# Row factors of the third graph layer computed on POOL as a power, with the engines' step order rewritten around it

## Chip, cores and metric

The kernel runs on one core of one Trainium2 chip. The metric is the device time of one execution in microseconds (us), lower is better. The engines are PE (matrix products and transposes), DVE (vector), ACT (activation functions), POOL (which here issues the indirect DMAs) and SP (which issues the direct DMAs).

## What is computed

Four graph layers follow one another on 50000 nodes of 128 features and 25000 edges, each followed by a residual sum and a normalisation over the features. The change touches the third layer (an attention layer whose own output is normalised once more before the residual):

```python
x_l = (x @ W_l + b_l).reshape(n, H, C)
x_r = (x @ W_r + b_r).reshape(n, H, C)
...
m = jax.nn.leaky_relu(x_j + x_r[tgt] + e_emb, NEG_SLOPE)
logits = jnp.einsum('ehc,hc->eh', m, att)
...
alpha = ex / (den[tgt] + 1e-16)
out = jax.ops.segment_sum(alpha[..., None] * x_j, tgt, num_segments=n)
...
out = jax.nn.gelu(out, approximate=False)
h = out + x
mu = jnp.mean(h, axis=-1, keepdims=True)
var = jnp.mean((h - mu) ** 2, axis=-1, keepdims=True)
return (h - mu) * jax.lax.rsqrt(var + LN_EPS) * ln_w + ln_b
```

## The kernel before

Every layer is a block of its own: the engines meet between layers. The third layer is `layer2`, and its tensors carry the prefix `g_` in the profile. Rows that belong to no layer of the change (`f_` is the last layer, `c_` the second) are not touched; the last layer, whose node pairs are loaded and scaled three steps ahead of its edges (`pairs_ahead = 3`), is the same text in both kernels.

`layer2` treats two kinds of rows. There are 49 node tiles of 1024 rows (two blocks of 512) and 49 edge tiles of 512 rows. Both are served by one loop over steps `c` from 0 to 63, written once for every engine, and each engine runs its instructions in exactly the order written; semaphores are the only other tie. In step `c` the node tile `g1 = c - 1` is activated by Gelu and centred, `g2 = c - 2` has its variance taken, and `g3 = c - 3` is scaled by its row factor, turned, given the affine weights and centred back. An edge tile is worked on twice: in step `c` its logits are computed as tile `c`, and eleven steps later (`lag = 11`) its softmax shares have come back from memory and it goes through the same Gelu, centre, scale, turn, affine chain as `e1 = c - 12` and `e3 = c - 14`. So there are three stretches: steps 0 to 10 with node tiles and edge logits only (here called the first stretch), steps 11 to 48 with everything (the joint stretch), and steps 49 to 63, the last of them (from 52) with edge tiles alone (the last stretch). Every seventh step has a part of the softmax in addition (`s1` and, one step later, `s2`).

The row factor is 1/sqrt(variance + eps). Per step ACT squares the centred rows (`sq1`, L1592), DVE adds the squares up (`var1`, `sums`, L1631), and ACT takes Ln and then Exp with scale -0.5 (`lnv1` L1608, `rstd1` L1613). Gelu and Ln/Exp are in different tables of ACT, so each step loads the Ln/Exp table (L1599) and, at the next Gelu, the Gelu table (L1558, in the last stretch L1563). ACT then multiplies the eight node row groups by their factors (`scale_block`, L1545) and DVE the edge block (`scaled`, L1627).

On PE a step is, in order: turn the node rows (L1405 into `psT`), the edge products (L1447, L1448), centre `gn` (L1410 into `psP`), centre `ge` (into `psU`), logits (L1471), turn the scaled nodes (L1405 `psT<-pre`), the second edge product (L1486), turn the scaled edges (L1405 into `psU` or `psZ`), centre the affine nodes (L1410 into `psP`), turn the next edge rows (L1405 `psT<-xd_xs`), centre the affine edges, node product (L1530). `turns` is one buffer of three blocks: `gn` and the affine node blocks use 0 and 1, `ge` and the affine edge block use 2.

POOL in `layer2` does nothing but issue eight indirect loads per step (L1332), `wait(pool, e_turned, now.n - 1)` ahead of them.

Of the kernel before, what the change touches and what calls it, by code (L numbers as in the profile page):

```python
# [1243 lines left out]
def layer2(nc, io, h):  # L1244
# [4 lines left out]
    with ExitStack() as ctx:  # L1249
# [25 lines left out]
        var1, lnv1, rstd1 = (sb(n, [P, 12]) for n in ("var1", "lnv1", "rstd1"))  # L1275
# [21 lines left out]
         ee_ready, pre1n_ready, pre1e_ready, sq1_ready, var1_ready, lnv1_ready, rstd1_ready, n1n_ready, n1e_ready, n1n_turned,  # L1297
# [6 lines left out]
             "pre1n_ready", "pre1e_ready", "sq1_ready", "var1_ready", "lnv1_ready", "rstd1_ready", "n1n_ready", "n1e_ready",  # L1304
# [9 lines left out]

        def edge_banks(c):
            return (psU[:, 0, :],) * 3 if c < STEPS else (psU[:, 0, :], psZ[:, 1, :], psZ[:, 0, :])
# [6 lines left out]
        def _(pool):  # L1323
            def step(t):
                now = t.tile(0)
                s = now.slot
                wait(pool, src_landed[s], 64 * now.half)
                wait(pool, dst_landed[s], 64 * now.half)
                wait(pool, e_turned, now.n - 1)
                for k, columns, landed in ((0, h.dst_row, dst_landed), (1, h.src_row, src_landed)):  # L1330
                    for j in range(4):
                        pool.indirect_dma_start(out=quarters(xd_xs[:, s, k, :])[j], out_offset=None, in_=table,  # L1332
                                                in_offset=edge_index(columns, now.n, j)).then_inc(landed[s], 16)

            run_steps(0, step)
# [66 lines left out]
        def _(pe):  # L1402
# [15 lines left out]

            def rows_of(dst, columns):
# [11 lines left out]
            for c in range(ends):  # L1431
                now, last = is_tile(c), is_tile(c - 1)
                g1, g3, e1, e3 = c - 1, c - 3, c - 1 - lag, c - 3 - lag
                sum_bank, turn_bank, out_bank = edge_banks(c)
# [15 lines left out]
                if is_tile(g1):  # L1450
# [3 lines left out]
                    ins.then_inc(en_ready, 1)  # L1454
                if is_tile(e1):
# [36 lines left out]
                if is_tile(e3):  # L1492
                    pe.wait_ge(n1e_ready, e3 + 1)
                    if c < STEPS:
                        pe.wait_ge(pre1e_ready, e1 + 1)
                    else:
                        pe.wait_ge(v_kept, STEPS)
                        wait(pe, affe_ready, e3)
                    turned_rows(turn_bank, pre1[:, g3 % 3, 2, :]).then_inc(n1e_turned, 1)
# [14 lines left out]
                if is_tile(e3):  # L1514
# [5 lines left out]
                    centred(out_bank, affT[:, 2, :]).then_inc(fe_ready, 1)  # L1520
# [14 lines left out]
        def _(act):  # L1535
# [15 lines left out]
            for c in range(ends):  # L1551
                now, last = is_tile(c), is_tile(c - 1)
                g1, g2, g3, e1, e2, e3 = c - 1, c - 2, c - 3, c - 1 - lag, c - 2 - lag, c - 3 - lag
                s1, (a, b) = run_at(c, runs + 1), blocks_of(g2)
# [5 lines left out]
                if is_tile(e1):  # L1560
                    act.wait_ge(agg_ready, e1 + 1)
                    wait(act, fe_ready, e1 - 2)
# [23 lines left out]
                if is_group(g2):  # L1586
                    if a == 0:
                        act.wait_ge(pre1n_ready, g2 + 1)
# [559 lines left out]
```

## Time and profile before

| | us |
|---|---|
| median of 3 runs | 3113.95 (3112.32 to 3114.8) |
| the profiled execution | 3120.47 |
| its span in the profile | 3118.6 |
| busy in it: PE, DVE, ACT, POOL | 2484.7, 2587.8, 2078.5, 1823.3 |

Busy is the time in which an engine worked on an instruction; the shares over the whole span average over four layers with different limits, so the prediction reads the stretches of `layer2` by themselves. In a timeline each row is an instruction or a run of equal ones: start, duration, engine, line, what it writes and reads, and in brackets how long the engine had been idle and what ended that.

### The profile page before, as it was taken

How to read it: one execution, taken by the hardware profiler on the slowest of the kernel's cores; microseconds unless marked ns; L12 is line 12 of the kernel's file. 1: busy time of each engine (PE TensorE's matmuls, PEld its weight loads, DVE VectorE, ACT ScalarE, POOL GpSimd, SP SyncE). 2: the span in 40 equal slices, each digit the busy share in tenths (PEclk: the TensorE clock that was granted, in tenths of full speed). 3: DMA queues.
4: the chain of work that ended last, by engine and by line, in shares of the span. 5: the costliest groups of instructions: out<-in, count | busy, mean ns of one | idle time of the engine just before them, and what ended most of it. 6: DMA issues, size and time to landing. Idle time of an engine off the chain costs nothing. (4 is left out here: it accounts for less than half of the span.)

```text
span 3118.6 us, 46608 instructions
## 1 busy us (share of the span) xinstructions
PE 2484.7 (80%) x14327; PEld 1752.4 (56%) x14327; DVE 2587.8 (83%) x3230; ACT 2078.5 (67%) x3724; POOL 1823.3 (58%) x1771
## 2 busy tenths in 40 slices
PE   7899999959999987888888589999999861435620
PEld 3466666637777765565666366777777651324420
DVE  6689999969999977999999557988999774999940
ACT  0167676736666656888888588999999863455520
POOL 4477777714434417777777365555555105777776
PEclk9999999979999998999999899999999955666765
DMA  7357676656777756777777447889988657995311
GB/s 211 117 168 225 219 223 220 221 166 203 218 219 219 218 168 203 236 233 230 231 232 231 126 139 186 214 201 234 225 219 203 179 147 230 296 283 165 95 53 39
DMA packets 495871, 611.80 MB, mean 196 GB/s; under 512 B 67257, under 2 KB 285827, under 8 KB 495500
## 3 DMA queue, kind: packets, MB, share of 16 engines
q1 hardware_dynamic: 433814, 495.64, 52.6%
q0 software_dynamic: 56480, 111.88, 13.8%
q8 instruction: 119, 1.95, 0.3%
q10 hardware_dynamic: 5334, 1.32, 0.2%
q14 instruction: 124, 1.02, 0.1%
HBM read 391.94 MB, written 220.55 MB: 196 GB/s over the span
## 5 line engine op out<-in xcount | busy, mean ns | idle before, releaser
L1332 POOL DMA_INDIRECT g_xd_xs<-table_x,dst_row x196 | 200.7, 1024 | 256.7 <-PE g_psT L1405 163.2
L781 POOL DMA_INDIRECT c_xs<-table_x,src_row x196 | 187.2, 955 | 261.0 <-PE c_psT L923 208.0
L1865 POOL DMA_INDIRECT f_rows<-table_x,src_row x196 | 191.3, 976 | 226.5 <-POOLq L1249 167.1
L771 POOL DMA_INDIRECT c_xs<-table_h,src_row x196 | 220.4, 1124 | 119.5 <-issue 78.8
L503 POOL DMA_INDIRECT xs<-in_x,src_i x196 | 227.1, 1159 | 86.2 <-issue 55.5
L488 POOL DMA_INDIRECT xd<-in_x,dst_i x196 | 216.5, 1105 | 95.0 <-issue 47.5
L1872 POOL DMA_INDIRECT out<-f_rows,end_i x196 | 196.5, 1003 | 66.5 <-issue 61.2
L1332 POOL DMA_INDIRECT g_xd_xs<-table_x,src_row x196 | 197.0, 1005 | 59.7 <-issue 59.7
L1916 PE MATMUL f_psT<-w_ident,f_rows 128*128 128x128 f32 x196 | 48.2, 391 | 219.8 <-DVE f_rows L2009 219.8
L771 POOL DMA_INDIRECT c_xd<-table_h,dst_row x196 | 185.0, 944 | 59.7 <-issue 59.7
L1410 PEld LDWEIGHTS g_psP<-w_center,g_turns 128*128 128x128 f32 x1568 | 186.0, 193 | 44.5 <-ACT g_turns L1558 27.6
L1410 PE MATMUL g_psP<-w_center,g_turns 128*128 128x128 f32 x1568 | 199.6, 281 | 6.1 <-ACT g_turns L1584 3.4
L1032 ACT ACTIVATE c_xo<-c_pre,c_rstd 128x128 f32<-128x128 f32 x588 | 182.0, 388 | 1.6
L1916 PEld LDWEIGHTS f_psT<-w_ident,f_rows 128*128 128x128 f32 x196 | 30.6, 194 | 232.2 <-DVE f_rows L2009 232.2
L1940 ACT ACTIVATE f_sqe<-f_rows 128x512 f32<-128x512 f32 x49 | 30.8, 630 | 159.6 <-DVE f_vare L1986 126.5
L953 PE MATMUL c_psV<-c_xsT,w_v 128*128 128x512 f32 x196 | 105.1, 618 | 35.6 <-DVE c_pv L1207 35.6
L1179 DVE TENSOR_TENSOR_SCAN c_m<-far,c_m,c_psA 128x512 f32<-128x512 bf16 x98 | 124.6, 1271 | 1.6 <-PE c_psA L958 1.6
L1410 PE MATMUL g_psU<-w_center,g_turns 128*128 128x128 f32 x672 | 100.9, 299 | 30.9 <-ACT g_turns L1563 30.9
L1213 DVE TENSOR_TENSOR_SCAN c_den<-c_c,c_den,c_p 128x512 f32<-128x512 f32 x96 | 122.2, 1273 | 0.0
L1219 DVE TENSOR_TENSOR_SCAN c_num<-c_c,c_num,c_pv 128x512 f32<-128x512 f32 x96 | 120.6, 1256 | 0.0
L1545 ACT ACTIVATE g_pre<-g_pre,g_rstd 128x128 f32<-128x128 f32 x392 | 119.3, 389 | 0.0
L1744 DVE TENSOR_TENSOR g_pre<-g_psP,g_xn 128x1024 f32<-128x1024 f32 x49 | 59.9, 1223 | 70.2 <-issue 39.0
(344 smaller groups left out, 8428.5 us busy)
## 6 DMA issues: line engine op xcount, KB each, us to landing
g_share<-shares SPq DMA_DIRECT2D x196, 192.0 KB
xn<-in_x SPq DMA_DIRECT2D x49, 512.0 KB
table_x<-xo SPq DMA_DIRECT2D x49, 512.0 KB
table_x1b<-xb SPq DMA_DIRECT2D x49, 512.0 KB, 4.9
c_xn<-table_x SPq DMA_DIRECT2D x49, 512.0 KB
table_h<-c_xo SPq DMA_DIRECT2D x49, 512.0 KB
c_xn<-table_h SPq DMA_DIRECT2D x49, 512.0 KB
c_x1r<-table_x1b SPq DMA_DIRECT2D x49, 512.0 KB
```

The costliest lines, as they stand in the source:

```text
L488: pool.indirect_dma_start(out=quarters(h.xd0[:, s, :])[j], out_offset=None, in_=io["x0"], in_offset=edge_index(h.dst_i, n, j)).then_inc(h. ...
L503: pool.indirect_dma_start(out=quarters(h.xs0[:, s, :])[j], out_offset=None, in_=io["x0"], in_offset=edge_index(h.src_i, n, j)).then_inc(h. ...
L771: pool.indirect_dma_start(out=quarters(rows[:, s, :])[j], out_offset=None, in_=table, in_offset=edge_index(columns, now.n, j)).then_inc(la ...
L781: pool.indirect_dma_start(out=quarters(xs[:, s, :])[j], out_offset=None, in_=table, in_offset=edge_index(h.src_row, now.n, j)).then_inc(sr ...
L1032: ins = nc.scalar.activation(quarters(xo[:, g.slot, j // 4, :])[j % 4], quarters(pre[:, g.slot, j // 4, :])[j % 4], ACT.Copy, scale=rstd[: ...
L1179: nc.vector.tensor_tensor_scan(m[:, s, 1:TILE + 1], h.far[:, here], psA[:, :], m[:, s, 0:1], ALU.add, ALU.max).then_inc(m_ready, 1)
L1213: nc.vector.tensor_tensor_scan(den[:, s, :], c[:, :], p[:, :], 0.0 if first else den[:, 1 - s, TILE - 1:TILE], ALU.mult, ALU.add).then_inc ...
L1219: nc.vector.tensor_tensor_scan(num[:, s, :], c[:, :], pv[:, :], 0.0 if first else num[:, 1 - s, TILE - 1:TILE], ALU.mult, ALU.add).then_in ...
L1332: pool.indirect_dma_start(out=quarters(xd_xs[:, s, k, :])[j], out_offset=None, in_=table, in_offset=edge_index(columns, now.n, j)).then_in ...
L1410: ins = nc.tensor.matmul(o, x, h.w["center"][:, :], start=True, stop=True)
L1865: pool.indirect_dma_start(out=quarters(rows[:, n, :])[j], out_offset=None, in_=table, in_offset=edge_index(h.src_row, n, j)).then_inc(src_ ...
L1872: pool.indirect_dma_start(out=io["out"], out_offset=edge_index(h.end_i, n, j), in_=quarters(rows[:, n, :])[j], in_offset=None, bounds_chec ...
```

## The change

The row factors of `layer2` are computed on POOL: `mean = var / 128 + eps`, then `mean` to the power -0.5 against a tile filled with -0.5. ACT's Ln and Exp of each step go, and with them the table loads, except around the softmax's Exp every seventh step. The square is taken one step earlier on ACT (tile `g1` at the end of its step instead of `g2`), the sums on DVE come before the first node sum instead of after the last, ACT scales the nodes first in its step, and in the steps that have edges alone PE turns the scaled edges ahead of the centring of `ge`, while the affine edge block goes to block 0 of `turns`. POOL issues the loads of tile `n` and then the factors of group `n - 4`, and its first loads now wait for `att_ready`.

```diff
         @block.gpsimd
         def _(pool):
-            def step(t):
-                now = t.tile(0)
-                s = now.slot
-                wait(pool, src_landed[s], 64 * now.half)
-                wait(pool, dst_landed[s], 64 * now.half)
-                wait(pool, e_turned, now.n - 1)
+            def gather(n):
...
+                wait(pool, e_turned, n - 1)
...
-            run_steps(0, step)
+            def factors(g, a, b):
+                pool.wait_ge(var1_ready, g + 1)
+                wait(pool, rstd1_ready, g)
+                nc.gpsimd.tensor_scalar(mean1[:, 4 * a:4 * b], var1[:, 4 * a:4 * b], 1.0 / P, EPS, ALU.mult,
+                                        ALU.add).then_inc(mean1_ready, 1)
+                pool.wait_ge(mean1_ready, g + 1)
+                wait(pool, n1n_ready, min(g, STEPS))
+                wait(pool, n1e_ready, g - lag)
+                nc.gpsimd.tensor_tensor(rstd1[:, 4 * a:4 * b], mean1[:, 4 * a:4 * b], minus_half[:, 4 * a:4 * b],
+                                        ALU.pow).then_inc(rstd1_ready, 1)
+
+            pool.wait_ge(att_ready, 1)
+            for n in range(STEPS + lag + 4):
+                if is_tile(n):
+                    gather(n)
+                if is_group(n - 4):
+                    factors(n - 4, *blocks_of(n - 4))
...
+                if is_tile(e3) and c >= first_alone:
+                    turn_sums(c)
                 if is_tile(e1):
                     pe.wait_ge(ge_ready, e1 + 1)
...
-                    centred(out_bank, affT[:, 2, :]).then_inc(fe_ready, 1)
+                    centred(out_bank, affT[:, affine_block(c), :]).then_inc(fe_ready, 1)
...
+                if is_tile(g3):
+                    act.wait_ge(rstd1_ready, g3 + 1)
+                    scale_block(g3, 0)
+                    scale_block(g3, 1).then_inc(n1n_ready, 1)
                 if is_tile(g1):
                     act.wait_ge(y_ready, g1 + 1)
...
-                    wait(act, fe_ready, e1 - 2)
+                    wait(act, fe_ready, min(e1 - 2, first_alone - 3 - lag))
+                    wait(act, ee_ready, e1)
                     nc.scalar.activation(ge[:, :], agg[:, e1 % 2, :], ACT.Gelu, bias=h.col("g_bias")).then_inc(ge_ready, 1)
-                if is_tile(g3):
-                    act.wait_ge(rstd1_ready, g3 + 1)
-                    scale_block(g3, 0)
-                    scale_block(g3, 1).then_inc(n1n_ready, 1)
...
-                if is_group(g1) and is_group(g2):
-                    nc.scalar.preload_act_table_set(LN_EXP)
+                if is_group(g1):
...
+                    nc.scalar.activation(sq1[:, a:b, :], pre1[:, g1 % 3, a:b, :], ACT.Square).then_inc(sq1_ready, 1)
                 if s1 is not None:
                     act.wait_ge(args_ready, s1 + 1)
+                    nc.scalar.preload_act_table_set(LN_EXP)
                     nc.scalar.activation(expo[:, :, :], expo[:, :, :], ACT.Exp).then_inc(exps_ready, 1)
...
-                    nc.scalar.activation(lnv1[:, 4 * a:4 * b], var1[:, 4 * a:4 * b], ACT.Ln, bias=h.eps[:, :],
-                                         scale=1.0 / P).then_inc(lnv1_ready, 1)
...
-                    nc.scalar.activation(rstd1[:, 4 * a:4 * b], lnv1[:, 4 * a:4 * b], ACT.Exp,
-                                         scale=-0.5).then_inc(rstd1_ready, 1)
...
+            nc.vector.memset(minus_half[:, :], -0.5)
...
+                if is_group(g2):
+                    dve.wait_ge(sq1_ready, g2 + 1)
+                    wait(dve, mean1_ready, g2)
+                    sums(var1[:, 4 * a:4 * b], sq1[:, a:b, :], var1_ready)
                 if is_tile(g1):
                     wait(dve, n1n_turned, g1 - 2)
...
-                if is_group(g2):
-                    dve.wait_ge(sq1_ready, g2 + 1)
-                    wait(dve, lnv1_ready, g2)
-                    sums(var1[:, 4 * a:4 * b], sq1[:, a:b, :], var1_ready)
```

`first_alone` is 52, and `affine_block(c)` is 2 before that step and 0 from it on.

ACT in one joint step without a softmax part, before, from the copy of the edge rows on:

```order
L1541 ACTIVATE g_edgeT<-g_psT 128x1024
L1608 ACTIVATE g_lnv<-g_var,eps 128x12
L1613 ACTIVATE g_rstd<-g_lnv 128x12
L1558 ACT_TABLE_LOAD
L1558 ACTIVATE g_turns<-g_psP,bl_out 128x1024
L1563 ACTIVATE g_turns<-g_agg,cols 128x512
L1545 ACTIVATE g_pre<-g_pre,g_rstd 128x128 x8
L1571 ACTIVATE g_nodeT<-g_psT 128x1024
L1575 ACTIVATE g_values<-g_psZ,cols 128x1024
L1580 ACTIVATE g_alike<-g_psA 128x256
L1584 ACTIVATE g_turns<-g_psT,cols 128x1024
L1592 ACTIVATE g_sq<-g_pre 128x1536
```

The same of the changed kernel, with its own line numbers:

```order
L1567 ACTIVATE g_edgeT<-g_psT 128x1024
L1571 ACTIVATE g_pre<-g_pre,g_rstd 128x128 x8
L1588 ACTIVATE g_turns<-g_psP,bl_out 128x1024
L1594 ACTIVATE g_turns<-g_agg,cols 128x512
L1598 ACTIVATE g_nodeT<-g_psT 128x1024
L1602 ACTIVATE g_values<-g_psZ,cols 128x1024
L1607 ACTIVATE g_alike<-g_psA 128x256
L1611 ACTIVATE g_turns<-g_psT,cols 128x1024
L1620 ACTIVATE g_turns<-g_psU,cols 128x512
L1628 ACTIVATE g_sq<-g_pre 128x1536
```

Ln, Exp and the load are gone between the edge copy and the Gelu, and the scaling of the nodes stands ahead of the Gelu.

DVE in a joint step, before, from the last sum of one step (L1807) on; L1744 is the first node sum and L1787 the second:

```order
L1807 TENSOR_TENSOR g_pre<-g_psU,g_x2e 128x512
L1730 TENSOR_TENSOR g_values<-g_values,g_share 128x1024
L1627 TENSOR_TENSOR g_pre<-g_pre,g_rstd 128x512
L1739 TENSOR_TENSOR g_values<-g_values 128x512
L1744 TENSOR_TENSOR g_pre<-g_psP,g_xn 128x1024
...
L1787 TENSOR_TENSOR g_pre<-g_psP,g_xn 128x1024
L1631 TENSOR_REDUCE g_var<-g_sq 128x12
L1796 SCALAR_TENSOR_TENSOR g_zsl<-g_low 128x512
```

The same place in the changed kernel (L1769 and L1812 are the two node sums):

```order
L1828 TENSOR_TENSOR g_pre<-g_psU,g_x2e 128x512
L1647 TENSOR_TENSOR g_pre<-g_pre,g_rstd 128x512
L1754 TENSOR_TENSOR g_values<-g_values,g_share 128x1024
L1760 TENSOR_TENSOR g_values<-g_values 128x512
L1651 TENSOR_REDUCE g_var<-g_sq 128x12
L1769 TENSOR_TENSOR g_pre<-g_psP,g_xn 128x1024
...
L1812 TENSOR_TENSOR g_pre<-g_psP,g_xn 128x1024
L1817 SCALAR_TENSOR_TENSOR g_zsl<-g_low 128x512
```

The sum of squares has moved from behind the second node sum to ahead of the first.

PE in steps that have edge tiles alone, two steps before:

```order
L1410 MATMUL g_psU<-w_center,g_turns 128x128 x4
L1405 MATMUL g_psZ<-w_ident,g_pre 128x128 x4
L1410 MATMUL g_psZ<-w_center,g_turns 128x128 x4
L1410 MATMUL g_psU<-w_center,g_turns 128x128 x4
L1405 MATMUL g_psZ<-w_ident,g_pre 128x128 x4
L1410 MATMUL g_psZ<-w_center,g_turns 128x128 x4
```

and in the changed kernel:

```order
L1425 MATMUL g_psZ<-w_ident,g_pre 128x128 x4
L1430 MATMUL g_psU<-w_center,g_turns 128x128 x4
L1430 MATMUL g_psZ<-w_center,g_turns 128x128 x4
L1425 MATMUL g_psZ<-w_ident,g_pre 128x128 x4
L1430 MATMUL g_psU<-w_center,g_turns 128x128 x4
L1430 MATMUL g_psZ<-w_center,g_turns 128x128 x4
```

The turn of the scaled edges now stands ahead of the centring of `ge`.

## Rows read from the trace of the kernel before

**Rows 1.** Windows: the three stretches; busy us (instructions) per engine, granted clock, DMA.

```profile
1780.00:1910.00 130.00, 116.13 (x714) 78.85 (x713) 73.10 (x104) 109.38 (x170) 85.68 (x89) 1.00 0.47 140
1937.00:2451.00 514.00, 499.67 (x3333) 369.10 (x3332) 459.53 (x619) 475.83 (x741) 277.77 (x270) 1.00 0.88 218
2470.00:2595.00 125.00, 75.51 (x347) 63.47 (x346) 76.88 (x112) 72.06 (x108) 0.00 (x0) 0.60 0.50 129
```

**Rows 2.** Groups of instructions, 1775 to 2595 us: busy, mean ns, idle before.

```profile
L1599 ACT ACT_TABLE_LOAD x59 | 75.7, 1283 | 1.1
L1558 ACT ACT_TABLE_LOAD x48 | 61.6, 1283 | 1.0
...
L1608 ACT ACTIVATE g_lnv<-g_var,eps 128x12 f32<-128x12 f32 (+2 forms) x60 | 18.1, 302 | 46.9 <-DVE g_var L1631 46.8
```

**Rows 3.** Timeline of one joint step: start, us, engine, line.

```profile
2223.95 2.05 PE L1410 MATMUL g_psP<-w_center,g_turns 128*128 128x128 f32 x16
...
2226.11 1.22 DVE L1787 TENSOR_TENSOR g_pre<-g_psP,g_xn 128x1024 f32<-128x1024 f32 x1 [1.00 <-PE g_psP L1410]
...
2227.25 1.74 DVE L1631 TENSOR_REDUCE g_var<-g_sq 128x12 f32<-128x1536 f32 x1
...
2229.59 1.28 ACT L1558 ACT_TABLE_LOAD   x1
...
2230.89 1.11 ACT L1558 ACTIVATE g_turns<-g_psP,bl_out 128x1024 f32<-128x1024 f32 x1
...
2235.95 1.06 PE L1405 MATMUL g_psT<-w_ident,g_pre 128*128 128x128 f32 x8 [0.39 <-issue]
...
2237.06 1.20 ACT L1584 ACTIVATE g_turns<-g_psT,cols 128x1024 f32<-128x1024 f32 x1
...
2238.31 2.05 PE L1410 MATMUL g_psP<-w_center,g_turns 128*128 128x128 f32 x16
```

**Rows 4.** Timeline of ACT: the Gelu of steps 11, 12 and 49.

```profile
1910.11 1.11 ACT L1558 ACTIVATE g_turns<-g_psP,bl_out 128x1024 f32<-128x1024 f32 x1
...
1923.32 1.12 ACT L1558 ACTIVATE g_turns<-g_psP,bl_out 128x1024 f32<-128x1024 f32 x1
...
2464.59 1.11 ACT L1558 ACTIVATE g_turns<-g_psP,bl_out 128x1024 f32<-128x1024 f32 x1
```

**Rows 5.** Timeline: POOL's loads of one joint step, and DVE beside them.

```profile
2183.65 0.94 POOL L1332 DMA_INDIRECT g_xd_xs<-table_x,dst_row  x1 [5.11 <-PE g_psT L1405]
...
2186.91 1.22 DVE L1730 TENSOR_TENSOR g_values<-g_values,g_share 128x1024 f32<-128x1024 f32 x1
...
2187.51 1.43 POOL L1332 DMA_INDIRECT g_xd_xs<-table_x,dst_row  x1 [0.30 <-issue]
...
2193.00 1.17 POOL L1332 DMA_INDIRECT g_xd_xs<-table_x,src_row  x1 [0.30 <-issue]
```

**Rows 6.** Timeline of the last stretch: one step, and sums L1807 of steps 51 and 60.

```profile
2508.66 0.68 DVE L1807 TENSOR_TENSOR g_pre<-g_psZ,g_x2e 128x512 f32<-128x512 f32 x1
...
2555.54 1.28 ACT L1563 ACT_TABLE_LOAD   x1 [0.36 <-PE g_psZ L1410]
...
2557.61 2.08 PE L1410 MATMUL g_psU<-w_center,g_turns 128*128 128x128 f32 x8 [2.15 <-ACT g_turns L1563]
...
2560.58 0.78 ACT L1596 ACTIVATE g_turns<-g_psZ,cols 128x512 f32<-128x512 f32 x1 [2.50 <-PE g_psZ L1405]
...
2563.57 1.28 ACT L1563 ACT_TABLE_LOAD   x1 [0.36 <-PE g_psZ L1410]
...
2579.65 0.69 DVE L1807 TENSOR_TENSOR g_pre<-g_psZ,g_x2e 128x512 f32<-128x512 f32 x1 [2.53 <-PE g_psZ L1410]
```

**Rows 7.** Timeline: the start of the layer, and POOL's operation of before.

```profile
0.94 0.34 POOL L425 IOTA i_rev_row<- 98x256 int32 x1
...
1756.83 0.94 POOL L1332 DMA_INDIRECT g_xd_xs<-table_x,dst_row  x1 [42.24 <-POOLq L789]
...
1757.91 0.17 DVE L1708 COPY g_att_a<-att_m 128x4 f32<-128x4 f32 x1
```

More of the change, by code:

```diff
@@ L1274, in layer2 @@
         gn, ge, affT = turns[:, 0:2, :], turns[:, 2, :], turns
-        var1, lnv1, rstd1 = (sb(n, [P, 12]) for n in ("var1", "lnv1", "rstd1"))
+        var1, mean1, rstd1, minus_half = (sb(n, [P, 12]) for n in ("var1", "mean1", "rstd1", "minus_half"))
         far, reach = sb("far", [P, runs, chunk], BF16), sb("reach", [P, runs, chunk])
@@ L1313, in is_group, with affine_block @@
             return 0 <= g < STEPS + lag
+        first_alone = STEPS + 3
+        def affine_block(c):
+            return 2 if c < first_alone else 0
         def edge_banks(c):
@@ L1323, in _ @@
         def _(pool):
-            def step(t):
-                now = t.tile(0)
-                s = now.slot
-                wait(pool, src_landed[s], 64 * now.half)
-                wait(pool, dst_landed[s], 64 * now.half)
-                wait(pool, e_turned, now.n - 1)
+            def gather(n):
+                s = n % 2
+                wait(pool, src_landed[s], 64 * (n // 2))
+                wait(pool, dst_landed[s], 64 * (n // 2))
+                wait(pool, e_turned, n - 1)
                 for k, columns, landed in ((0, h.dst_row, dst_landed), (1, h.src_row, src_landed)):
@@ L1417, in turn_edges, with turn_sums @@
                 turned_rows(psT[:, 1, :], xd_xs[:, n % 2, 1, :]).then_inc(e_turned, 1)
+            def turn_sums(c):
+                e1, g3, e3 = c - 1 - lag, c - 3, c - 3 - lag
+                pe.wait_ge(n1e_ready, e3 + 1)
+                if c < STEPS:
+                    pe.wait_ge(pre1e_ready, e1 + 1)
+                else:
+                    pe.wait_ge(v_kept, STEPS)
+                    wait(pe, affe_ready, e3)
+                turned_rows(edge_banks(c)[1], pre1[:, g3 % 3, 2, :]).then_inc(n1e_turned, 1)
             def rows_of(dst, columns):
@@ L1491, in _ @@
                     rows_of(psA[:, 0, :], [c_here[:, chunk - 1:chunk], d_here[:, chunk - 1:chunk]]).then_inc(d_rows, 1)
[L1492 to L1499, printed above, removed]
+                if is_tile(e3) and c < first_alone:
+                    turn_sums(c)
                 if s1 is not None:
@@ L1726, in _ @@
                     running_maximum(s1)
+                if is_tile(e3):
+                    dve.wait_ge(rstd1_ready, g3 + 1)
+                    scaled(pre1[:, g3 % 3, 2:3, :], pre1[:, g3 % 3, 2:3, :], rstd1[:, 8:12], 1, n1e_ready)
                 if is_tile(e0):
@@ L1730, in _ @@
                     nc.vector.tensor_tensor(v, v, share[:, e0 % 2, 1:3, :], ALU.mult).then_inc(weighed, 1)
-                if is_tile(e3):
-                    dve.wait_ge(rstd1_ready, g3 + 1)
-                    scaled(pre1[:, g3 % 3, 2:3, :], pre1[:, g3 % 3, 2:3, :], rstd1[:, 8:12], 1, n1e_ready)
                 if s2 is not None:
```

38 lines of the change are left out of this document (17 added, 21 removed).

## The prediction

> **What bounds the kernel now.** I read the windows of the third layer first, because the change lies wholly inside it, then the groups of instructions for what each edit removes, then the timeline of one step per stretch, to find the loop of waits that sets the step. [rows 1] are the three stretches. In the joint stretch PE is busy 499.7 of 514 us (97%), ACT 93%, DVE 89%, POOL 54%: three engines are nearly full, so taking time from one of them is worth only the distance to the next. In the first stretch PE has 89%, ACT 84%, DVE 56%. In the last, no engine has over 62%, and the granted clock is 0.60, that is mostly the lower level of 1.2 GHz: this stretch is a chain of waits, and PE's products in it cost twice.
>
> The steps come from [rows 4]: 13.21 us in the first stretch (step 11 to 12), and (2464.59 - 1923.32) / 37 = 14.63 us in the joint one. [rows 3] show what sets it. From the start of the second node centring (PE, 2223.95) it goes to the second node sum on DVE (2226.11), to the sum of squares (2227.25, 1.74 us), to Ln and Exp on ACT, to the table load (2229.59, 1.28 us), to the Gelu (2230.89), through ACT's scaling and copies to the affine activation (2237.06), and to the same PE instruction (2238.31): 14.36 us, closed without a gap worth naming. ACT's mean wait for the sum of squares is 46.9 / 60 = 0.78 us a step [rows 2]. So in the joint stretch the loop is PE, DVE, ACT in turn, with PE just under it.
>
> **What the change does, part by part.**
>
> Ln, Exp and the loads. 59 + 48 loads of 1.283 us and 11 more at the edge Gelu [rows 2, 6] become one pair per softmax run, 14 in all with the first Gelu counted; with Ln at 0.30 and Exp at about two thirds of that, ACT loses some 3.1 us a step and its wait of 0.78. In the joint stretch ACT falls from 13.5 to about 10.6 us a step, so it no longer bounds. The loop above is cut in two places: the sum of squares is no longer between the node sum and the next Gelu, and the factor gets a step of slack on POOL.
>
> What takes over in the joint stretch. PE is next. As the windows count it, it is busy 0.972 x 14.63 = 14.2 us a step [rows 1, 4], which leaves 0.4 us at most. That busy time has slack in it that the profile hides, since ends are modelled: the turn of the scaled nodes waited at 2235.95 for ACT's node copy (0.39 us idle [rows 3]), and ACT gets there about two us earlier in the new order, because the scaling no longer sits behind a load. Below is 13.2 us, DVE's 0.89 x 14.63 = 13.1 and a little for its semaphores; above is 14.36, no gain. I take 13.95 for a step without a softmax part, 0.4 less. Three of seven steps carry or feel the softmax parts, which are chains on DVE, and I give them 0.25. (4 x 0.4 + 3 x 0.25) / 7 = 0.34 us, times 37 steps: -13 us.
>
> POOL's two operations. No row shows a tensor operation of POOL with inputs. From below: its iota took 0.34 us [rows 7], twice that is 0.7. From above: an indirect DMA takes it up to 1.43 us when something holds it up, [rows 5], twice that and two waits of 0.3 are 3.5 us. 128 x 12 elements are a small load and nearer to the iota; I take F = 1.6 us for both with their waits. In the joint stretch POOL issues its loads in 10.5 us (2183.65 to 2194.17) and had then waited 5.11 us for PE [rows 5], so 1.6 lies in that idle time. What waits for the factor is ACT's scaling, first in its next step, and behind it everything on ACT; the sums are ready long before the loads are all issued, so the factor is there 10.5 + 1.6 = 12.1 us after the loads began and about two us before ACT wants it.
>
> First stretch. Its step could fall to PE's 0.89 x 13.21 = 11.8 us [rows 1, 4]. But POOL needs 10.5 + 0.3 + 1.6 = 12.4 us there, as the factors stand in the same queue, somewhat less where loads aren't stretched. I take 12.3, a gain of 0.9 over nine steps: -8 us.
>
> Last stretch. Step 51 to 60 are nine steps in 2579.65 - 2508.66 = 71.0 us, 7.9 each. [rows 6] show one: load 1.28, Gelu, PE 2.08, turn, ACT 0.78, PE 2.08, load again, 8.03 in all. The ring closes because Gelu and affine edges share a block of `turns`; the change gives them two, turns first, and loads nothing. What stays is edge scaling on DVE (0.68 by the same shape as L1807), turn 0.9 (2559.69 to 2560.58), two PE groups of 2.08 behind each other, and the last sum 0.69: 6.4 us. That is 1.5 x 9 = -13.5. At the higher clock PE's two groups would halve and DVE's own work would bound the step near 5.5; at no gain it stays 7.9. In steps 49 to 51, from 2464.59 [rows 4] to 2508.66 [rows 6], 44.1 us, the path loses a load (1.28), Ln and Exp (0.5) and the sum of squares (1.74): 3.5 each, -10.5. Together -24.
>
> The costs. The first loads wait for `att_ready`: the copy that gives it ends at 1758.08, the loads began at 1756.83 [rows 7], and PE's first turn waits for them: +1.3 us, with nothing to hide it. The extra memset of DVE is under 0.1. One more configuration instruction of POOL stands ahead of its first factor; POOL's start in this layer, which has one too, was 0.6 us behind the others, and it falls into idle time.
>
> Sum: -13 - 8 - 24 + 1.3 = -44 us. The profiled execution was 3120.5 (span 3118.6), 6.5 above the median of the runs, so it goes to about 3076, and the median from 3114 to **3070**.
>
> **A rule that speaks against it.** The long load of 1.43 us in [rows 5] against 0.94 for its neighbours lies beside L1730, a DVE product of two operands in SBUF: so POOL and DVE disturb one another here already. The Trainium skill, "SBUF — State Buffer", section "Who interferes with whom", says that a DVE instruction with two SBUF inputs and a GpSimd instruction that reads SBUF exclude each other for a whole instruction. The new POOL operations read SBUF, the loads' descriptors mostly write. By that rule either side can be held: this is the second rival.
>
> **Rivals.**
> 1. POOL's power is dear, and the kernel gets slower. The place is POOL's queue: a step can't be shorter than 10.8 + F. Speaking for it: a power isn't a simple operation, and no row prices it. Against: only 12 elements per partition. With F = 5.3 (two operations, each 1.43 and held by a DVE product of 1.22 us [rows 5]) the step is 16.1 in both stretches: (16.1 - 14.6) x 37 + (16.1 - 13.2) x 9 = +81; in the last stretch, where 3.3 us lie between sum and scaling, its nine steps gain nothing and -8 remains. +74: 3188. It decides from F = 4 on: 9 x 1.6 + 37 x 0.15 + 1 - 18 is about +3.
> 2. POOL and DVE exclude each other. F stays small, but each joint step loses about 1 us of DVE, which has 1.5 us to spare and has it at other places. Then the joint stretch gains nothing or loses 0.7 x 37 = 26, and the rest gives its 31: 3083 to 3109, a case that can end within what counts as no change.
> 3. PE alone bounds the joint stretch, as its busy share says: 14.2 us is all it gives, with nothing in softmax steps, 0.1 x 37 = 4. Then -35: 3079, nearly the forecast.
> 4. More than forecast: DVE's 13.3 us becomes the joint step and the last stretch keeps the higher clock: -37 - 33 - 12 = -80: 3034.
>
> **How the numbers follow.** Forecast with rival 3: 0.72; rival 4 or near it 0.09; rival 2 0.09, a third of it within 0.2%; rival 1 0.10, nearly all slower. 0.2% is 6 us, about what a measurement of this kernel can tell from no change. Faster 0.86, same 0.04, slower 0.10. The range 3038 to 3106 leaves out rival 1 and the tips of 2 and 4.
>
> **What would show it.** ACT loads of the layer fall from 118 to 15 or less. POOL shows two short operations per step with a sum under 2 us, and its queue doesn't end the wait of ACT's scaling. The joint step is near 14.3 us on average and PE stays at 0.97 busy or more; the first stretch near 12.3 with POOL nearly without idle time; the last near 6.4 a step. I am wrong if POOL's operations take over 3.5 us, if DVE's products beside them lengthen, or if PE's groups in the joint stretch turn out to have more hidden waiting than 0.4 us a step.

## The result, and the profile after

The changed kernel takes 3101.67 us (median of 5 runs, 3096.52 to 3104.76) beside 3113.95 for the kernel before on the same chip: ratio 0.995, 95% interval 0.9939 to 0.9961. Measured again on another chip it took 3095.95 beside 3113.71: 0.9941, interval 0.9928 to 0.9955. So it is 12 to 18 us faster where 44 were forecast.

The third layer, from its first table load to that of the layer behind it, took 838.9 us in the profile of before and 816.1 after. By parts, marked by the starts of the node Gelu (n-th tile) and of the last edge node sum, in us:

| part of the layer | before | forecast | after | both again |
|---|---|---|---|---|
| start to Gelu 1 | 25.51 | +1.3 | 27.95 (+2.4) | 25.67, 27.87 |
| Gelu 1 to 3 | 21.42 | with the next | 29.52 (+8.1) | 21.46, 30.05 |
| Gelu 3 to 12 | 120.20 | -8 | 119.34 (-0.9) | 120.22, 119.24 |
| Gelu 12 to 49 (37 joint steps) | 541.27 | -13 | 534.65 (-6.6) | 541.26, 534.43 |
| Gelu 49 to the last edge sum | 126.09 | -24 | 100.23 (-25.9) | 123.82, 101.09 |

The rest of the layer is 4.43 us in both. The windows of [rows 1] after the change, at the same times and with the same columns:

```profile
1780.00:1910.00 130.00, 109.44 (x650) 73.42 (x649) 67.65 (x98) 81.31 (x131) 97.59 (x99) 0.95 0.40 123
1937.00:2451.00 514.00, 497.59 (x3364) 370.94 (x3362) 461.21 (x622) 391.28 (x613) 406.27 (x351) 1.00 0.91 220
2470.00:2595.00 125.00, 63.75 (x371) 57.09 (x370) 87.53 (x121) 47.90 (x70) 32.80 (x42) 0.74 0.66 175
```

ACT's busy time in the joint stretch fell from 93% to 76%, POOL's rose from 54% to 79%, and PE stayed at 97%, but less was won than ACT gave up. The groups of instructions in the layer, ACT's table loads against [rows 2] and POOL's new operations:

```profile
L1588 ACT ACT_TABLE_LOAD x7 | 9.0, 1283 | 0.1
L1631 ACT ACT_TABLE_LOAD x7 | 9.0, 1283 | 13.3 <-DVE g_expo L1687 13.3
...
L1347 POOL TENSOR_TENSOR g_rstd<-g_mean,g_minus_half 128x12 f32<-128x12 f32 x38 | 91.1, 2396 | 3.2
L1347 POOL TENSOR_TENSOR g_rstd<-g_mean,g_minus_half 128x8 f32<-128x8 f32 x11 | 18.3, 1667 | 0.9
L1342 POOL TENSOR_SCALAR g_mean<-g_var 128x12 f32<-128x12 f32 x38 | 11.1, 293 | 38.7 <-DVE g_var L1651 37.7
L1347 POOL TENSOR_TENSOR g_rstd<-g_mean,g_minus_half 128x4 f32<-128x4 f32 x11 | 11.1, 1007 | 0.9
```

The loads are gone as forecast (16 left). But the seven that remain before the softmax's Exp have 13.3 us of waiting for DVE ahead of them, and the power takes 2.40 us for 12 columns: F is 2.40 + 0.29 and gaps, 3.0 us, against 1.6 forecast.

The first loss is at the third Gelu, 20.34 us behind the second where it had been 11.22. ACT, and the end of POOL's queue before it (start, duration, ..., idle time and what ended it):

```profile
1804.40 1.02 ACT L1567 ACTIVATE g_edgeT<-g_psT 128x1024 f32<-128x1024 f32 x1 [1.59 <-PE g_psT L1425]
1814.10 2.44 ACT L1571 ACTIVATE g_pre<-g_pre,g_rstd 128x128 f32<-128x128 f32 x8 [8.68 <-POOL g_rstd L1347]
1816.45 1.09 ACT L1588 ACTIVATE g_turns<-g_psP,bl_out 128x1024 f32<-128x1024 f32 x1
```
```profile
1803.49 0.94 POOL L1336 DMA_INDIRECT g_xd_xs<-table_x,dst_row  x1 [0.30 <-issue]
...
1811.01 0.95 POOL L1336 DMA_INDIRECT g_xd_xs<-table_x,src_row  x1 [0.30 <-issue]
1812.08 0.22 POOL L1342 TENSOR_SCALAR g_mean<-g_var 128x8 f32<-128x8 f32 x1
1812.39 1.68 POOL L1347 TENSOR_TENSOR g_rstd<-g_mean,g_minus_half 128x8 f32<-128x8 f32 x1
```

On DVE the sums of the first tile had been ready since 1796.23:

```profile
1795.02 1.21 DVE L1651 TENSOR_REDUCE g_var<-g_sq 128x8 f32<-128x1024 f32 x1
```

POOL comes to them 15.9 us later, behind the loads of the fifth tile, and ACT, which scales first in its step, holds everything back until then.

The second loss is in each softmax step of the joint stretch, 17.3 to 17.8 us long where it had been 15.63. A softmax step on ACT in the kernel before, with the load done by the time DVE's exponents came:

```profile
2180.89 1.28 ACT L1599 ACT_TABLE_LOAD   x1
2182.43 0.48 ACT L1602 ACTIVATE g_expo<-g_expo 128x336 f32<-128x336 f32 x1 [0.26 <-DVE g_expo L1667]
```

and one after:

```profile
2190.05 1.47 ACT L1628 ACTIVATE g_sq<-g_pre 128x1536 f32<-128x1536 f32 x1
2192.96 1.28 ACT L1631 ACT_TABLE_LOAD   x1 [1.44 <-DVE g_expo L1687]
2194.26 0.48 ACT L1632 ACTIVATE g_expo<-g_expo 128x336 f32<-128x336 f32 x1
...
2195.55 2.44 ACT L1571 ACTIVATE g_pre<-g_pre,g_rstd 128x128 f32<-128x128 f32 x8
2198.00 1.28 ACT L1588 ACT_TABLE_LOAD   x1
2199.30 1.11 ACT L1588 ACTIVATE g_turns<-g_psP,bl_out 128x1024 f32<-128x1024 f32 x1
```
```profile
2200.47 1.72 PE L1430 MATMUL g_psP<-w_center,g_turns 128*128 128x128 f32 x13 [1.70 <-ACT g_turns L1588]
```

ACT waits 1.44 us for DVE's exponents with the old table in, and loads only then. Behind that stand the scaling (2.44), the second load and the Gelu, and PE waits 1.70 us for the Gelu. The 37 joint steps hold five softmax steps. These five and the five that follow them took 153.0 us before and 156.5 after, so they lost 3.4 us; the other 27 steps, called ordinary here, went from 388.3 to 378.2 and won 10.1.

The ordinary steps could have won more. The factor, which was to be ready two us before ACT wants it, is ready just as ACT takes it: in 20 of the 37 joint steps ACT's scaling starts less than 0.1 us behind the power, and nine times from 1940 to 2400 ACT had waited for it, 7.4 us in all. One of these nine, with POOL's power ahead of it, and the row of the waits (us in total, times, longest):

```profile
2074.43 2.29 POOL L1347 TENSOR_TENSOR g_rstd<-g_mean,g_minus_half 128x12 f32<-128x12 f32 x1
2076.76 2.45 ACT L1571 ACTIVATE g_pre<-g_pre,g_rstd 128x128 f32<-128x128 f32 x8 [0.78 <-POOL g_rstd L1347]
```
```profile
ACT g_pre L1571 <- POOL g_rstd L1347: 7.4, 9, 1.3
```

### The profile page after: what moved, and what is told of

Its sections match the earlier page's. It is cut to its first block and busy times, and to the rows that moved or that the text cites. A ratio compares the mean times of both kernels' runs of the same rounds, so it can differ in the third digit from the quotient of the medians.

```text
span 3099.9 us, 46510 instructions
## 1 busy us (share of the span) xinstructions
PE 2460.4 (79%) x14327; PEld 1739.5 (56%) x14327; DVE 2586.2 (83%) x3231; ACT 1926.8 (62%) x3501; POOL 1987.3 (64%) x1891
## 5 line engine op out<-in xcount | busy, mean ns | idle before, releaser
L1336 POOL DMA_INDIRECT g_xd_xs<-table_x,dst_row x196 | 226.4, 1155 | 122.6 <-issue 57.7
L1571 ACT ACTIVATE g_pre<-g_pre,g_rstd 128x128 f32<-128x128 f32 x392 | 119.6, 389 | 16.4 <-POOL g_rstd L1347 16.1
L1347 POOL TENSOR_TENSOR g_rstd<-g_mean,g_minus_half 128x12 f32<-128x12 f32 (+2 forms) x60 | 120.5, 2008 | 5.0
L1769 DVE TENSOR_TENSOR g_pre<-g_psP,g_xn 128x1024 f32<-128x1024 f32 x49 | 59.8, 1221 | 69.3 <-issue 52.7
```

## The experiments

The ratios are to the kernel before on the same chip; times of parts come from each run's own trace.

**1. The table load ahead of the wait.**

```diff
-                    act.wait_ge(args_ready, s1 + 1)
                     nc.scalar.preload_act_table_set(LN_EXP)
+                    act.wait_ge(args_ready, s1 + 1)
```

> The changed kernel with one line moved: in each of the seven softmax steps ACT loads the Ln/Exp table before it waits for DVE's arguments instead of after. Theory A (the loads of the softmax steps stand on the path: such steps took 17.3 to 17.8 us in the joint stretch against 15.6 before the change, and ACT stood idle 1.44 us for DVE before the load at 2192.96): each of the seven steps loses up to 1.28 us, the kernel 6 to 9 us, to about 3094, and the row of the load no longer has idle time for DVE ahead of it. Rival B (POOL's queue sets these steps too, so ACT's time is free): within 2 us of the changed kernel.

3091.57 us, ratio 0.9921 (0.9904 to 0.9937). The same step on ACT:

```profile
2184.74 1.47 ACT L1628 ACTIVATE g_sq<-g_pre 128x1536 f32<-128x1536 f32 x1
2186.23 1.28 ACT L1630 ACT_TABLE_LOAD   x1
2187.56 0.48 ACT L1632 ACTIVATE g_expo<-g_expo 128x336 f32<-128x336 f32 x1
```

The softmax steps fall to 16.1 to 16.6 us, the one in the first stretch from 16.02 to 14.74, the joint stretch to 529.58. Wait and load now run side by side: the idle time of 1.44 us is gone. Theory A holds. In the joint stretch the softmax steps and their followers win 7.0 us, 1.4 per softmax step, and the ordinary steps give 1.9 of it back, with ACT waiting for POOL's factor ten times, 9.3 us.

**2. The first two factors ahead of the loads of tiles 4 and 5.**

```diff
             for n in range(STEPS + lag + 4):
+                if n in (4, 5):
+                    factors(n - 4, *blocks_of(n - 4))
                 if is_tile(n):
                     gather(n)
-                if is_group(n - 4):
+                if is_group(n - 4) and n not in (4, 5):
```

> The changed kernel, but POOL computes the factors of groups 0 and 1 before the loads of tiles 4 and 5 instead of after them. Theory C (the first factors queue behind five tiles of loads: ACT stood idle 8.68 us for them, and step 2 to 3 took 20.3 us against 11.2 before): ACT's wait falls under 1 us, and the kernel loses 7 to 9 us, to about 3093. Rival D (POOL is behind from the start and the time lost there only moves: the loads of tiles 4 and 5 come late instead, since POOL issues one tile in 10 us and has to wait for the sums): 0 to 3 us gained.

3100.59 us, 0.9951 (0.9934 to 0.9967). The stall isn't gone; it stands two steps later. POOL's operations without its loads:

```profile
1799.52 0.74 POOL L1342 TENSOR_SCALAR g_mean<-g_var 128x8 f32<-128x8 f32 x1
1800.34 1.68 POOL L1347 TENSOR_TENSOR g_rstd<-g_mean,g_minus_half 128x8 f32<-128x8 f32 x1
1812.67 0.22 POOL L1342 TENSOR_SCALAR g_mean<-g_var 128x8 f32<-128x8 f32 x1
1812.98 1.68 POOL L1347 TENSOR_TENSOR g_rstd<-g_mean,g_minus_half 128x8 f32<-128x8 f32 x1
1835.85 0.20 POOL L1342 TENSOR_SCALAR g_mean<-g_var 128x8 f32<-128x8 f32 x1
```

The third factor comes 23 us after the second, since two tiles' loads now stand between them, and ACT waits 8.4 us for it. Gelu 1 to 12 takes 148.7 us (148.9 in the changed kernel, 141.6 before). So it isn't a matter of the first factors: with loads ahead of factors in POOL's queue, the layer pays once for a factor that comes a tile's loads late, wherever the order begins. Rival D was right.

**3 and 4. The power's price: a product in its place, and the power twice.** The third run multiplies where the power should be, so its row factors aren't those of the reference; the fourth computes one more power into a spare tile that nobody reads.

```diff
-                                        ALU.pow).then_inc(rstd1_ready, 1)
+                                        ALU.mult).then_inc(rstd1_ready, 1)
```

> The changed kernel with the power replaced by a product, so the row factors are wrong and the output with them; instructions, waits and order are the same. It prices the power (2.4 us for 12 columns, 1.67 for 8, 1.01 for 4). Theory E (POOL's queue bounds first and joint stretch: eight loads 10.8 us and 3.0 us for the factors): a product takes about 0.3 us, a step of POOL falls by 2.1 us, and the joint step falls from 14.45 to PE's 13.6 to 14.0 on average, the first stretch from 12.72 to 11.8 to 12.2 a step, together -20 to -35 us, to 3065 to 3082. Rival F (PE alone bounds the joint stretch, POOL has room): -5 to -12, from the first stretch and the first factors alone.

```diff
+                nc.gpsimd.tensor_tensor(spare[:, 4 * a:4 * b], mean1[:, 4 * a:4 * b], minus_half[:, 4 * a:4 * b], ALU.pow)
                 nc.gpsimd.tensor_tensor(rstd1[:, 4 * a:4 * b], mean1[:, 4 * a:4 * b], minus_half[:, 4 * a:4 * b],
```

> The changed kernel with a second power of the same size into a spare tile ahead of the real one; the output is unchanged. Theory E (POOL bounds): the 37 joint steps grow by nearly the whole 2.4 us, the first stretch by 1.7 a step, together +90 to +110 us, to about 3200, and POOL waits for PE nowhere. Rival F (POOL has slack): the slack is used up first, +30 to +60.

With the product: 3092.51 us, 0.9932 (0.9914 to 0.9949). Its price, by groups:

```profile
L1347 POOL TENSOR_TENSOR g_rstd<-g_mean,g_minus_half 128x12 f32<-128x12 f32 x38 | 11.8, 311 | 3.2
```

2.1 us less a step gives only 534.65 - 530.93 = 3.7 us over 37 joint steps: the ordinary ones win 5.3, those with and after a softmax part lose 1.6. ACT waits for POOL's factor nowhere in the joint stretch and mostly takes it some 2 us after it is ready, and most ordinary steps come to 13.70 us, with PE counted busy throughout. The steps without softmax in the first stretch stay at 12.7, and the third Gelu is still late (18.84 us). Rival F is about right: PE's own 13.70 lies just under what POOL allowed, so the power itself took little. With two powers: 3172.23 us, 1.0181 (1.0164 to 1.0198), joint stretch 598.56. One step of POOL in it:

```profile
2084.51 1.59 POOL L1336 DMA_INDIRECT g_xd_xs<-table_x,dst_row  x1 [0.18 <-issue]
...
2096.29 0.22 POOL L1342 TENSOR_SCALAR g_mean<-g_var 128x12 f32<-128x12 f32 x1
2096.59 2.30 POOL L1345 TENSOR_TENSOR g_spare<-g_mean,g_minus_half 128x12 f32<-128x12 f32 x1
2098.88 2.32 POOL L1348 TENSOR_TENSOR g_rstd<-g_mean,g_minus_half 128x12 f32<-128x12 f32 x1
2101.38 1.49 POOL L1336 DMA_INDIRECT g_xd_xs<-table_x,dst_row  x1 [0.18 <-POOL g_rstd L1348]
```

Here POOL has no idle time beyond the 0.2 to 0.3 us between its instructions; 12 us of loads and 5 of factors make most ordinary steps 15.8 to 16.9 us. The second power costs 63.9 / 37 = 1.7 us a step of its 2.3, and in the ordinary steps alone 2.2, nearly all of it: in the changed kernel POOL had next to no room in them, and PE's 13.70 was just beneath. Theory E is right on what sets these steps; its +90 to +110 us was too high, the layer grew by 75.

**5. The last stretch's order undone.**

```diff
-        first_alone = STEPS + 3
+        first_alone = 2 * STEPS
...
-                            act.wait_ge(ee_ready, e1 + 1)
+                            act.wait_ge(ee_ready, min(e1 + 1, STEPS))
```

> Two parts of the change for the last stretch are undone: the turn of the edge sums stands again behind the other turns, and the affine edges keep one block. The loads and the sum of squares stay gone. The last stretch took 126.1 us before and 100.2 in the changed kernel. Theory G (the -26 us come mostly from the loads, Ln, Exp and the sum of squares that left the path): it stays within 5 us of 100, the kernel near 3105. Rival H (the ring through the shared block, one load in each step of 8.03 us, has to be cut as well): a step is 8.03 - 1.28 = 6.75 against the 5.6 measured, so +12 us over eleven steps, the kernel near 3114, as slow as the one before.

3105.22 us, 0.9965 (0.9951 to 0.9979). The stretch takes 108.25 us, 8.0 more than in the changed kernel, between G's 5 and H's 12. Seven of its steps are 6.73 to 6.75, H's number. PE and ACT in one, then in the changed kernel:

```profile
2532.55 0.78 ACT L1620 ACTIVATE g_turns<-g_psZ,cols 128x512 f32<-128x512 f32 x1 [3.03 <-PE g_psZ L1425]
...
2533.38 2.08 PE L1430 MATMUL g_psZ<-w_center,g_turns 128*128 128x128 f32 x8 [0.87 <-ACT g_turns L1620]
...
2536.35 2.05 PE L1430 MATMUL g_psU<-w_center,g_turns 128*128 128x128 f32 x8 [0.90 <-ACT g_turns L1594]
```
```profile
2535.12 1.06 PE L1430 MATMUL g_psU<-w_center,g_turns 128*128 128x128 f32 x8
2535.32 0.78 ACT L1620 ACTIVATE g_turns<-g_psZ,cols 128x512 f32<-128x512 f32 x1 [1.18 <-PE g_psZ L1425]
...
2536.15 1.05 PE L1430 MATMUL g_psZ<-w_center,g_turns 128*128 128x128 f32 x7
```

In the old order each centring waits 0.9 us for ACT and lasts 2.05 to 2.08; in the new one, PE goes from one to the next, and part of them last 1.05. The granted clock from 2475 to 2575 is 0.61 there and 0.77 in the changed kernel. So of the 25.9 us, 18 come from the loads, Ln, Exp and the square, and 8 from the order. The 8 are rather 4 to 8: from the sum of step 51 to the last one it took 62.6 us in the changed kernel, 62.9 to 66.4 in the other kernels with the new order and 63.6 in the second profile of the changed one, against 70.4 here.

**6. The attention wait behind the first loads.**

```diff
-            pool.wait_ge(att_ready, 1)
             for n in range(STEPS + lag + 4):
+                if n == 4:
+                    pool.wait_ge(att_ready, 1)
```

> POOL's wait for the attention copy stands ahead of its first factors and not ahead of its first loads. The time from the layer's start to its first Gelu was 25.5 us before and 27.95 in the changed kernel. Theory I (the wait ahead of the loads costs all of that): -2.4 us, the first Gelu 25.5 us after the start. Rival J (the first Gelu waits for other parts of the layer's start too): under 1 us. The total can hardly show it; the time to the first Gelu does.

Start to first Gelu 26.59 us, 1.36 less and still 1.1 more than before: between I and J. The wait costs what the prediction gave it (1.3); what makes the other 1.1 stays open. The whole (3096.07 us, 0.9938, 0.9918 to 0.9957) can't show it.

**7. Gelu ahead of the scaling, on top of run 1.**

```diff
-                if is_tile(g3):
-                    act.wait_ge(rstd1_ready, g3 + 1)
-                    scale_block(g3, 0)
-                    scale_block(g3, 1).then_inc(n1n_ready, 1)
...
+                if is_tile(g3):
+                    act.wait_ge(rstd1_ready, g3 + 1)
+                    scale_block(g3, 0)
+                    scale_block(g3, 1).then_inc(n1n_ready, 1)
```

> On top of the load ahead of the wait (3091.6 us): ACT computes the node and edge Gelu first and scales the older tile's nodes behind it, as the kernel before did. Theory K (PE's centring waits for the Gelu 23 times, 21.8 us in 450, and the scaling of 1.2 to 2.4 us stands ahead of it): the Gelu comes earlier by the scaling, the joint stretch loses up to 20 us, the kernel goes to 3075 to 3085. Rival L (the step hangs on the scaling, through the turn and the affine copies to PE, which in the first stretch waits 1.26 us a step for them): the first stretch goes from 12.7 to near 13.2 a step, and the joint one gains nothing or loses up to 0.5 a step: 3095 to 3112.

3084.24 us, 0.9897 (0.9878 to 0.9916); the joint stretch takes 522.63 us, 7.0 less than in run 1, the layer 803.1 (810.5 in run 1). Most steps without a softmax part are 13.69 to 13.70, and the softmax steps 15.5:

```profile
2176.17 1.28 ACT L1630 ACT_TABLE_LOAD   x1
2177.59 0.48 ACT L1632 ACTIVATE g_expo<-g_expo 128x336 f32<-128x336 f32 x1
...
2179.00 1.28 ACT L1584 ACT_TABLE_LOAD   x1
2180.82 1.11 ACT L1584 ACTIVATE g_turns<-g_psP,bl_out 128x1024 f32<-128x1024 f32 x1 [0.54 <-PE g_psP L1556]
```

Now the Gelu waits for PE's product, not PE for the Gelu. Theory K's number comes, and L's loss in the first stretch doesn't (12.7 a step as before). But K's reason isn't where the gain lies. The 21.8 us that it starts from belong to PE's weight loads; PE itself waited 7.8 us for the Gelu. And by kinds of steps, in us (the second profiles gave 153.0 and 388.2 for the kernel before, 155.8 and 378.6 for the changed one):

| joint stretch | softmax steps and the steps after them (10) | ordinary (27) |
|---|---|---|
| before | 153.0 | 388.3 |
| changed | 156.5 | 378.2 |
| load ahead of the wait (run 1) | 149.5 | 380.1 |
| product (run 3) | 158.0 | 372.9 |
| two powers (run 4) | 162.1 | 436.4 |
| Gelu ahead of the scaling (run 7) | 150.6 | 372.0 |

Against run 1 the softmax steps win nothing (the step falls to 15.5, the one after it grows from 13.6 to 14.6); all of the gain, 8.1 us, is in the ordinary steps. There ACT had waited 9.3 us for POOL's factor in run 1; now the scaling comes later in ACT's step, finds the factor about 2 us old or older, and never waits. The product, with the old order on ACT, reaches the same 13.70 a step. So a factor that comes earlier and a scaling that comes later give the same, and what the ordinary steps had lost was the wait for the factor.

**8. Factors ahead of the loads in every step** (on the changed kernel alone).

```diff
             for n in range(STEPS + lag + 4):
-                if is_tile(n):
-                    gather(n)
                 if is_group(n - 4):
                     factors(n - 4, *blocks_of(n - 4))
+                if is_tile(n):
+                    gather(n)
```

> In every step POOL computes the factors ahead of that step's loads, and not only at the start. Theory M (the 9.1 us that the third Gelu waits come from one tile's loads of some 9 to 10 us that stand between sum and factor, once, and with the order turned they never do): -9 us, 3093, the wait doesn't come back later, since the next loads are always behind a factor that is ready. Rival N (POOL then waits for each sum with its loads unissued, and the tiles arrive later): steps of the first stretch grow from 12.7 towards 14 and the joint ones by what POOL waits: 3100 to 3130.

3098.21 us, 0.9943 (0.9924 to 0.9962). Both are right, each in its stretch: Gelu 1 to 12 falls from 148.9 to 142.1 us, and the joint stretch grows from 534.7 to 540.5. The last stretch varies besides, and the layer takes 818.5 us, 2.4 more than in the changed kernel.

**9 and 10. All four edits together; and with factors ahead only for tiles up to 15.** Runs 1, 6, 7 and 8 in one kernel, and the same with this loop:

```diff
+                if is_tile(n) and n > 15:
+                    gather(n)
                 if is_group(n - 4):
                     factors(n - 4, *blocks_of(n - 4))
-                if is_tile(n):
+                if is_tile(n) and n <= 15:
                     gather(n)
```

> Four edits together: load ahead of the wait, Gelu ahead of the scaling, the attention wait behind the first loads, and factors ahead of loads in every step. The first three alone should give 3084.2 - 1.4 = 3082.8. The fourth gave -6.8 us between Gelu 1 and 12 and +5.8 in the joint stretch. Theory O (the +5.8 is POOL's own and stays): 3082, joint stretch 528. Rival P (the +5.8 came from ACT's order, scaling ahead of the Gelu, and is gone with it): 3076, joint stretch 523.

> As the run of four edits, but factors stand ahead of loads only up to the sixteenth tile, and behind them from there. Under theory O this keeps the -6.8 and pays no 5.8, but once a stall where the order turns over, since two tiles' loads then stand ahead of one factor: up to 5 us. That gives 3076 to 3081, and it beats the run of four edits by 1 to 6 us. Under rival P it is behind that run by the stall, 0 to 5 us.

All four: 3088.49 us, 0.9918 (0.9906 to 0.993), joint stretch 534.80, 12.2 more than in run 7, so worse than O, and P falls. Two rows of its waits from 1940 to 2400 (us in total, times, longest):

```profile
POOL g_mean L1342 <- DVE g_var L1652: 28.0, 20, 2.8
...
PE g_psT L1426 <- DMA g_xd_xs<-table_x,src_row: 10.2, 9, 1.9
```

The changed kernel has neither row in that stretch: here POOL waits for sums with its loads unissued, and PE then waits for the loads. The tenth: 3079.98 us, 0.9884 (0.9869 to 0.9899), the lowest of all. Gelu 1 to 12 is 3.7 us shorter than in run 7 and the joint stretch 4.4 longer, with one step of 20.0 us where the order turns over. Run 7 has 12.75 us from the tenth Gelu to the eleventh, this run 18.64, in which PE waits 4.06 us for a tile's loads to land; the ninth, in the same order up to there, had 13.43, so why isn't shown. In time it can't be told from run 7 (layer 801.3 against 803.1).

**11 and 12. Both kernels again, for second profiles.**

> The kernel before itself, for a second profile of it. The third layer, from its first table load to that of the layer behind it, took 838.9 us in the first profile and 816.1 in that of the changed kernel, -22.8, while the medians are only 12.3 us apart. In the eight profiles of other versions the median minus the layer's time lies between 2278.7 and 2281.6 (2285.5 for the changed one), and for the kernel before it is 2275.0. Theory Q (the first profile of before caught a layer some 6 us slower than usual): 833 us now. Rival R (the layer takes 839 always and another part of the kernel is what differs between profile and median): 838 to 840, and the rest of the span 5 us shorter than the 2279.7 of the first profile.

> The changed kernel itself, for a second profile and a measurement beside the kernel before on one chip. Theory Q: the layer takes 816 us again, within 1.5, and the ratio is 0.995, within 0.0015. Rival S (its layer varies from execution to execution as well): 819 us or more.

The kernel before: layer 836.9 us, its parts in the table above, ratio to itself 1.0006 (0.9997 to 1.0015). Q falls, the layer wasn't slow by chance; R holds for the layer, but the rest of the span was 2283.1, not 5 us shorter. The changed kernel: 817.1. Gelu 1 to 49 repeats within 0.4 us in both; what varies is the last stretch (2.3 us in the kernel before) and the other layers. The profiled execution of before was each time some 6 us above its median (3120.5, 3121.8), that of the changed kernel at its median; why, stays open. In the second measurement layer and whole agree: 3115.98 and 3095.95 us are 20.0 apart, the layers 19.7. In the first they don't, 12.3 against 22.8. So the layer's gain is 20 to 23 us, and how much of it arrives in the whole is known only as 12 to 20.

## Why the prediction failed, step by step

**The first stretch: -8 forecast, +7.2 measured (Gelu 1 to 12).** The step that failed is "POOL needs 10.5 + 0.3 + 1.6 = 12.4 us there": a rate was worked out and no start. The sentence that "the factor is there 10.5 + 1.6 = 12.1 us after the loads began and about two us before ACT wants it" takes for granted that the sums are ready long before the loads are all issued and POOL is abreast; at the layer's beginning POOL's queue is a tile's loads behind the sum. That cost 8.1 us, and runs 2 and 8 show that the order in POOL's queue is the cause. From Gelu 3 to 12 only 0.9 us were won of the 8: the step after the stall was 1.4 longer than before, the softmax step 1.6 (run 1 takes 1.3 of that back), and the other seven won 3.9, about 0.5 each where 0.9 was forecast. Their steady length came to 12.7, not 12.3, with F = 2.3 for 8 columns, and POOL doesn't set it: with the product, and with ACT's order turned (run 7), it is 12.75 as well. In all three PE is busy 11.7 us of it, waits 0.43 for the affine activation (L1611) and 0.60 for the second node sum (L1812), and each of these two had itself just waited for PE. So it is PE with two short round trips, 11.7 + 1.03; no run took them out.

**The joint stretch: -13 forecast, -6.6 measured.** With the two orders on ACT turned back it gives 541.27 - 522.63 = 18.6 us (run 7), at a steady 13.70 against 13.95 forecast, so the 97% of PE did hide more waiting than the 0.4 us that I gave it (rival 3, PE's floor at 14.2, is refuted). Two steps failed. The first is "three of seven steps carry or feel the softmax parts, ... and I give them 0.25": the softmax step got 1.7 to 2.2 us longer, and with the step after it the five lost 3.4 us in place of a gain of 2.5. The diff showed why and I gave it no price: the preload moved from ahead of the wait to behind it, 1.4 us a softmax step, 7.0 in the stretch by run 1, which is more than the whole loss. The second is the sentence on the factor, "about two us before ACT wants it": loads and factors took POOL 13.1 to 14.6 us in nearly every joint step and not 12.1 (F was 1.4 more, and eight loads took up to 11.8 where one step's 10.5 had been read), ACT's scaling stood first in a shorter step, and the two us were gone; of the signs that I had named, POOL's queue did end waits of ACT's scaling. That cost the ordinary steps 5 to 6 us (runs 3 and 7). Their 10.1 us still met the forecast for them (about 10), and that is luck: the floor of PE was lower than I said by about as much as the wait for the factor took.

**F: 1.6 forecast, 3.0 measured.** A mis-sized term. A power costs much more than a product (2.40 against 0.31 us), which the iota couldn't show. It stayed under the point of 4 us from which rival 1 decides, and was worth 3.7 us. Rival 1's formula was right for the joint stretch: with two powers F is about 5.3, and its step of 16.1 was met by 16.2 on average. Its 3188 against 3172 is less exact: the first stretch, with 8 columns, had steps of 13.6 to 14.0, and the last one won 22 us where rival 1 left 8.

**The last stretch: -24 forecast, -25.9 and -22.7 measured.** The total is right and its mechanism too (run 5: without the new order steps are 6.75, and the loads, Ln, Exp and the square are worth 18), but the two terms in it were each off: -10.5 forecast and -6.5 measured up to the sum of step 51, -13.5 forecast and -19.4 measured behind it, where I left out the last two steps and where eleven steps of 4.1 to 6.75 came in place of 6.4. The shortest have products of 1.05 us, the length at the higher clock, which was rival 4's part. That the two errors cancel is luck.

**The layer's start: +1.3 forecast, +2.4 measured.** The term that I priced is right (1.36 by run 6); another 1.1 us isn't explained.

Together: +1.1 for the start, +15.2 for the first stretch, +6.4 for the joint, -1.9 for the last make 20.8 us of the 21 between -44 and the layer's -22.8. The rest to the medians lies outside the layer and stays open: I took the 6.5 us by which the profiled execution stood over the median to be in both kernels, and it was not.

**Rival 2, POOL and DVE holding each other.** DVE's sums and products keep their times beside a power; the power doesn't. Two of them in the changed kernel, the first with the DVE product of two SBUF tensors (`g_ew`, `g_values`) that runs as it starts:

```profile
2017.10 0.72 DVE L1788 SCALAR_TENSOR_TENSOR g_zw<-g_ew,cols,g_values 128x512 f32<-128x512 f32 x1
2017.26 2.73 POOL L1347 TENSOR_TENSOR g_rstd<-g_mean,g_minus_half 128x12 f32<-128x12 f32 x1
...
2059.96 2.29 POOL L1347 TENSOR_TENSOR g_rstd<-g_mean,g_minus_half 128x12 f32<-128x12 f32 x1
```

Of the 38 powers of 12 columns 29 took 2.27 to 2.30 us and nine 2.72 to 2.74, and those nine all start beside L1788, which takes 0.72 us with or without them. In run 3 nine of the 38 products start so as well, and take 0.64 us against 0.21. By the Trainium skill, "SBUF — State Buffer", section "Who interferes with whom", such a product and a GpSimd instruction lock each other out. The trace agrees for POOL's side, at 0.43 us a time and not for as long as L1788 still ran (0.56). It comes to 4 us in all, and in each of the nine ACT took the factor 0.4 to 2.2 us later still, so it cost nothing; that DVE gave way is seen nowhere.

## What to carry to other kernels

When an in-order engine gets a new task behind a batch of its own (here a factor behind eight loads), work out the first tiles too, not only the rate: the task is late by the batch, once, and turning the order round can cost more later than it saves. When a table load is taken out of most steps, look where the remaining ones stand: ahead of a wait they are free, behind it they cost in full. And when a value is handed from one in-order engine to another, look at the slack and not only at who waits longest: here the consumer took the factor as it came, and both a cheaper factor and a consumer placed later in its step gave the same 13.70 us.

## What the runs showed of the hardware

POOL's power took 1.01, 1.67 and 2.29 us for 4, 8 and 12 columns of 128 partitions, about 0.16 us a column, where its product took 0.20, 0.20 and 0.21; the means of 2.40 and 0.31 for 12 columns hold the nine that were held up by 0.43 us. A table load took 1.28 us, and the next activation started 0.02 us behind it (2198.00 and 2199.30). In the last stretch, the same centring on PE took 2.05 to 2.08 us with 0.9 us of waiting ahead of each, and part of them 1.05 us when PE went on without a gap, at granted clocks of 0.61 and 0.77 over the stretch: turning the order of two groups round gave 4 to 8 us, of which the runs don't separate the closed gaps from the shorter products.
